# Summing attention and graph-convolution blocks of edges with one scan each instead of one vector operation per edge

## What is computed

```
L0: segment_sum(exp(-w)[:, None] * x[dst], src)
L1: MLP over segment_sum, max and mean of edge_attr_32 by src
L2: twice   h = x @ W
            out = segment_sum(h[src] * norm[:, None], dst) + b
L3: attention, 4 heads of 16:
    attn = leaky_relu(a_src[src] + a_dst[dst] + edge_attr @ W_edge)
    attn = exp(attn - max over dst);  attn /= sum over dst
    out  = segment_sum(h[src] * attn, dst)
```

## Time and profile before

| | |
|---|---|
| median of 3 timed runs | 10099.72 us |
| span of the profiled execution | 11181.7 us |
| busy in it: POOL, DVE, PE, ACT | 7106.9, 4736.9, 1801.6, 1142.1 us |
| ranking pass, first to last scatter issue | 511.8 to 2881.5 us |
| c1, first to last gather issue | 3850.1 to 6017.3 us |
| c2, first to last gather issue | 6222.7 to 8389.4 us |
| attention, first to last gather issue | 8707.2 to 10966.1 us |

### The profile page before, as it was taken

One profiled execution on the slowest core, in us unless ns is written; L12 is line 12 of the kernel. 1 busy time (PEld: TensorE's weight loads), 2 busy tenths in 40 slices (PEclk: granted clock), 3 DMA queues, 4 the chain that ended last, 5 costly groups with the idle time before them and its releaser, 6 DMA issues.

```text
span 11181.7 us, 57120 instructions
## 1 busy us (share of the span) xinstructions
PE 1801.6 (16%) x9285; PEld 1516.5 (14%) x9285; DVE 4736.9 (42%) x20005; ACT 1142.1 (10%) x2728; POOL 7106.9 (64%) x6884
## 2 busy tenths in 40 slices
PE   8744444444000400000000000000001000000000
PEld 7633333333000300000000000000000000000000
DVE  8855555555797422222221222222224344444446
ACT  0143434343000100000000000000000000000000
POOL 0566666666201377777776677777777776666766
PEclk7755555555555555555555555555555555555555
DMA  5144444444575111111111111111111222222221
GB/s 224 57 129 122 129 124 126 124 127 122 204 273 203 32 50 46 48 46 48 46 48 37 50 46 48 46 48 46 48 46 30 54 53 58 53 58 55 56 55 44
DMA packets 570444, 911.29 MB, mean 81 GB/s; under 512 B 333435, under 2 KB 348228, under 8 KB 544824
## 3 DMA queue, kind: packets, MB, share of 16 engines
q1 hardware_dynamic: 350264, 652.74, 17.3%
q0 software_dynamic: 219904, 255.88, 10.8%
HBM read 494.12 MB, written 414.02 MB: 81 GB/s over the span
## 4 chain that ended last, share of the span: by engine, by line
DVE 34%; issue 28%; another core or an unknown queue 17%; POOL 16%; PE 3%; DMA 1%; ACT 1%; DVEq 0%; SPq 0%; POOLq 0%; ACTq 0%
DVE arena_a L1495 16%; POOL arena_a L641 15%; DVE arena_b L1112 4%; DVE arena_a L1110 3%; DVE arena_b L1125 3%; DVE arena_a L1425 3%; POOL arena_a L610 2%; PE bank L811 2%; DVE arena_b L1056 1%; DVE arena_b L1093 1%; PE bank L916 1%; DVE arena_a L1625 0%; PE bank L890 0%; DMA arena_a<-in_a 0%
## 5 line engine op out<-in xcount | busy, mean ns | idle before, releaser
L641 POOL DMA_INDIRECT arena_a<-table_c,decay x3136 | 3284.6, 1047 | 1257.6 <-issue 1051.2
L1495 DVE SCALAR_TENSOR_TENSOR arena_a<-arena_a,same_dst 128x64 f32<-128x64 f32 x3134 | 891.5, 284 | 3449.5 <-DVE arena_a L1495 2713.2
L591 POOL DMA_INDIRECT by_src<-arena_b,idx_blk x1568 | 1570.8, 1002 | 885.8 <-issue 449.4
L641 POOL DMA_INDIRECT arena_a<-table_at,decay x1568 | 1556.8, 993 | 703.8 <-issue 468.4
L1110 DVE SCALAR_TENSOR_TENSOR arena_a<-arena_a,same_dst 128x64 f32<-128x64 f32 x1567 | 441.9, 282 | 711.1 <-remote 547.7
L864 PE MATMUL bank<-ident,chunk_end 128*64 128x128 f32 (+2 forms) x8 | 2.7, 442 | 4416.0 <-DVEq L973 4416.0
L864 PEld LDWEIGHTS bank<-ident,chunk_end 128*64 128x64 f32 (+2 forms) x8 | 1.4, 240 | 4416.6 <-DVEq L973 4416.6
L1112 DVE SCALAR_TENSOR_TENSOR arena_b<-arena_a,src_f,before 128x128 bf16<-128x128 f32 x1568 | 543.7, 347 | 37.4 <-issue 37.4
L850 PE MATMUL bank<-hrows 98*128 98x128 f32 x1568 | 404.0, 440 | 659.5 <-DVE arena_b L1125 331.9
L850 PE MATMUL bank<-hrows,arena_a 98*128 98x128 f32 x1568 | 403.3, 438 | 658.0 <-DVE arena_b L1125 347.4
L753 ACT ACTIVATE arena_b<-arena_a,decay 128x64 f32<-128x64 f32 x1568 | 394.2, 334 | 972.5 <-remote 610.2
(11 more groups left out here) (279 smaller groups left out, 4845.9 us busy)
## 6 DMA issues: line engine op xcount, KB each, us to landing
arena_a<-ids_rows SPq DMA_DIRECT2D x98, 1024.0 KB
states_src<-arena_a SPq DMA_DIRECT2D x98, 1024.0 KB
states_c<-arena_a SPq DMA_DIRECT2D x196, 512.0 KB
hrows<-by_src SPq DMA_DIRECT2D x98, 776.0 KB, 6.1
states_at<-arena_a SPq DMA_DIRECT2D x98, 576.0 KB
x_at_start<-arena_a SPq DMA_DIRECT2D x7, 7168.0 KB, 49.0
arena_a<-x_at_start SPq DMA_DIRECT2D x98, 512.0 KB
arena_a<-table_c,decay POOLq DMA_INDIRECT x3136
```

Source lines behind the costliest of these rows:

```text
L591: pool.indirect_dma_start(out=by_src, out_offset=AT(ap=idx_blk[r][:, k:k + 1], axis=0), in_=rows[r][:, k, :], in_offset=None)\
L641: pool.indirect_dma_start(out=gb[r][:, k * w:(k + 1) * w], out_offset=None, in_=table[g], in_offset=AT(ap=src_i[:, n * J + k:n * J + k + 1 ...
L1495: ins = v.scalar_tensor_tensor(out=st[h][:, k * D:(k + 1) * D], in0=old, scalar=same_dst[:, e:e + 1], in1=gb[r][:, k * D:(k + 1) * D], op0 ...
```

## The change

Every block of the three passes is now laid out feature by feature: 64 (c1, c2) or 68 (attention) rows of J + 1 = 17 slots. Slot 0 holds what is carried from the block before, slots 1 to 16 the edges; a mask of the same layout holds same_dst in slots 1 to 16 and 0 in slot 0, so that one TENSOR_TENSOR_SCAN over all 64 * 17 = 1088 or 68 * 17 = 1156 columns starts again at each feature. The buffers `in0`, `in1`, `mask0`, `mask1` lie at the end of arena_b, `sums0`, `sums1` in arena_a.

In c1 and c2, ACT spreads the mask (`mask_spread`, 1024 columns), turns the gathered block from edge-major to feature-major (1024 columns) and, after the scan, turns the sums back into `st` (`rows_back`, 1024 columns). DVE does one scan and one copy of 64 columns that carries the last slot over. POOL waits for `row_turned` of ACT instead of `state`. In attention the weighing writes the feature-major order itself, the exponentials of ACT go straight to it, POOL waits for `weighed`, the scan takes the place of the 33 operations, and steps 0 to 2 of the next block's scores (step 2 waits for the next block's gathers) are issued before it, steps 3 to 6 behind it. The products `run` are gone.

```diff
-        run = {2 ** level: digits[o, w][:, :].bitcast(f32)[:, 0:NBLK * J // 2]...
+        by_feature = carve(arena_b[:, KN * W01 - 4 * W3 * (J + 1):],
+                           [(f"{name}{h}", W3 * (J + 1)) for name in ("mask", "in") for h in range(2)])
...
+        def features(name, w):
+            return by_feature[name][:, 0:w * (J + 1)].rearrange("p (f j) -> p f j", j=J + 1)
...
-                    if n >= R:
-                        pool.wait_ge(s("state"), upto(g, "state") + n - R + 1)
+                    if n >= R and g == "at":
+                        pool.wait_ge(s("weighed"), n - R + 1)
+                    elif n >= R:
+                        pool.wait_ge(s("row_turned"), upto(g, "row_turned") + n - R + 1)
...
+        def mask_spread(act, g, n):
+            w = W3 if g == "at" else D
+            if n >= 2:
+                act.wait_ge(s("summed"), upto(g, "summed") + n - 1)
+            act.activation(features(f"mask{n % 2}", w)[:, :, 1:J + 1], bf(same_dst[:, n * J:(n + 1) * J], w), ACT.Copy)\
+               .then_inc(s("mask_spread"), 1)
+
+        def rows_back(act, g, n):
+            w, row = (W3, W3S) if g == "at" else (D, D)
+            act.wait_ge(s("summed"), upto(g, "summed") + n + 1)
+            if n >= 2:
+                act.wait_ge(s(f"stored{n % 2}"), upto(g, f"stored{n % 2}") + 16 * (n // 2))
+            act.activation(st[n % 2][:, 0:J * row].rearrange("p (j f) -> p j f", f=row)[:, :, 0:w],
+                           features(f"sums{n % 2}", w)[:, :, 1:J + 1].rearrange("p f j -> p j f"), ACT.Copy)\
+               .then_inc(s("state"), 1)
+
+        def conv_act(act, g):
+            act.wait_ge(s("masks_zeroed"), 1)
+            for n in range(NBLK):
+                r = n % R
+                mask_spread(act, g, n)
+                act.wait_ge(s(f"gathered{r}"), upto(g, f"gathered{r}") + (n // R + 1) * (16 * J))
+                act.activation(features(f"in{n % 2}", D)[:, :, 1:J + 1],
+                               gb[r][:, 0:J * D].rearrange("p (j f) -> p f j", f=D), ACT.Copy)\
+                   .then_inc(s("row_turned"), 1)
+                if n:
+                    rows_back(act, g, n - 1)
+            rows_back(act, g, NBLK - 1)
...
-                    for k in range(J):
...
-                        ins = v.scalar_tensor_tensor(out=st[h][:, k * D:(k + 1) * D], in0=old,
...
+                    v.wait_ge(s("mask_spread"), upto(g, "mask_spread") + n + 1)
+                    v.wait_ge(s("row_turned"), upto(g, "row_turned") + n + 1)
+                    flat = slice(0, D * (J + 1))
+                    v.tensor_tensor_scan(by_feature[f"sums{h}"][:, flat], by_feature[f"mask{h}"][:, flat],
+                                         by_feature[f"in{h}"][:, flat], 0.0, ALU.mult, ALU.add).then_inc(s("summed"), 1)
+                    if n + 1 < NBLK:
+                        v.wait_ge(s("summed"), upto(g, "summed") + n + 1)
+                        v.tensor_copy(features(f"in{1 - h}", D)[:, :, 0], features(f"sums{h}", D)[:, :, J])\
+                            .then_inc(s("row_carried"), 1)
...
-                hview = by_head(g3)[:, :, :, 0:HD]
-                v.tensor_tensor(hview, hview, ex_e.rearrange("p j (c o) -> p j c o", o=1)
+                v.tensor_tensor(weighed(n)[:, :, 0:HD, 1:J + 1].rearrange("p c d j -> p j c d"),
+                                by_head(g3)[:, :, :, 0:HD], ex_e.rearrange("p j (c o) -> p j c o", o=1)
                                 .to_broadcast([P, J, HEADS, HD]), ALU.mult).then_inc(s("weighed"), 1)
                 if ahead:
-                    score_step(n + 1, 0)
+                    for step in range(3):
+                        score_step(n + 1, step)
                 v.wait_ge(s("weighed"), n + 1)
-                sums_of(n, g3, late["tmp"], s3[:, :, 0:W3], n + 1 if ahead else None)
+                if n >= 2:
+                    v.wait_ge(s("state"), upto("at", "state") + n - 1)
+                v.tensor_tensor_scan(by_feature[f"sums{h}"], by_feature[f"mask{h}"], by_feature[f"in{h}"], 0.0,
+                                     ALU.mult, ALU.add).then_inc(s("summed"), 1)
+                if ahead:
+                    for step in range(3, 7):
+                        score_step(n + 1, step)
```

More of the change, by code:

```diff
@@ L59 @@
 ORDER = dict.fromkeys(ADDED, PASSES)
-ORDER.update(dict.fromkeys((*(f"gathered{r}" for r in range(R)), "table", "table_out", "chain"),
-                           CONVS))
+ORDER.update(dict.fromkeys((*(f"gathered{r}" for r in range(R)), "table", "table_out", "row_turned", "row_carried",
+                            "mask_spread", "summed"), CONVS))
 ORDER.update(dict.fromkeys(("onehots", "onehots_used"), ("dst", "src")))
@@ L1416, in _ @@
             tell("table")
[L1418 to L1440, removed]
-                    for k in ks:
-                        if k // span % 2:
-                            last = join(k, made[:, k // span * span - 1, :],
-                                        run[span][:, n, k // (2 * span) * span + k % span:][:, 0:1], k % span == 0)
-                    return last
-                def score(step):
-                    if scored:
-                        score_step(scored, step)
-                first, second = range(half), range(half, J)
-                joined("first", join(0, carried, same_dst[:, e:e + 1], True))
-                joined("second", pairs(range(half + 1, J, 2)))
-                pairs(range(3, half, 2))
-                score(1)
-                after_half("first")
-                joined("first", join(1, made[:, 0, :], same_dst[:, e + 1:e + 2], True))
-                after_half("second")
-                joined("second", level(2, second))
-                score(2)
-                after_half("first")
-                joined("first", level(2, first))
-                after_half("second")
-                joined("second", level(4, second))
-                score(3)
-                after_half("first")
-                joined("first", level(4, first))
-                score(4)
-                after_half("second")
-                after_half("first")
-                level(half, range(half, half + 4))
-                score(5)
-                level(half, range(half + 4, J)).then_inc(s("state"), 1)
-                score(6)
@@ L1521, in conv_nodes @@
                 link(v.tensor_tensor(rows3, rows3, per_node(dinv, p, D), ALU.mult))
-            for span, product in run.items():
-                uppers = same_dst[:, :].rearrange("p (m two k) -> p m two k", two=2, k=span)[:, :, 1, :]
-                to = product.rearrange("p n (m k) -> p (n m) k", k=span)
-                link(v.tensor_copy(to, uppers))
-                for k in range(1, span):
-                    link(v.tensor_tensor(to[:, :, k], to[:, :, k], to[:, :, k - 1], ALU.mult))
+            for h in range(2):
+                link(v.memset(by_feature[f"mask{h}"], 0.0))
+            tell("masks_zeroed")
             conv("c1")
@@ L1565, in _ @@
             link(v.memset(late["mx"], 0.0))
-            for h in range(2):
-                link(v.memset(msk[h], 0.0))
             tell("at_begun")
```

71 lines of the change are left out of this document (26 added, 45 removed).

## The result

| | before | after |
|---|---|---|
| median of 4 timed runs | 10099.69 us | 10624.1 us |
| lowest to highest | 10092.31 to 10106.65 | 10619.74 to 10627.47 |

The changed kernel is slower: ratio 1.052, 95% interval 1.0505 to 1.0535, or 524 us. The profiled execution of after took 10624.95 us and its span is 10622.7 us. The profile of before had a span of 11181.7 us. Profiled again in experiment 1, the same kernel has a span of 10104.8 us, and experiments 9 to 11 meet a chip on which it takes 11112.54 us; most likely the profile of before comes from such a chip, though its chip isn't on record.

The account below looks back on a forecast made before the run. The prediction took POOL's issuing of indirect transfers to bound all three passes. Its terms, 382 + 143 - 3 = +522 us on 10099.7, gave 10620 us (5.2% slower), with a range of 10400 to 10800.

Parts of the forecast that it names:

- the pace of 1.40 us: In the profile of before, a dependent DVE step every 1.40 us instead of 0.32; claimed absent from timed runs.
- Term 1: c1 and c2: removing DVE's chain of 16 steps, 5.1 us a block, is worth nothing; likewise attention's 33 operations.
- Term 2: ACT in c1 and c2: three operations of 1.13 us, 3.4 us of a 20 us block, covered even at 7 us.
- the prediction's own sign: Check on ACT's work: its estimate is wrong if an ACT operation takes over 2 us.
- Term 3, c1 and c2: The long scan holds a POOL gather issued under it: 1.95 us a block in 196 blocks, +382 us.
- Term 3, attention: The scan holds a gather for 1.7 us, short operations give back 0.24: 1.46 in 98 blocks, +143 us.
- Term 4: Moved waits of POOL and the carry copy after the scan: 0, at most 0.15 us a block, 44 us in all.
- Term 5: Ends of passes: nothing in c1 and c2, -3 us in attention.
- The profiled execution: The profiled span should fall by about 140 us, to 11040, while timed runs get slower.
- Rival A: DVE's slow pace is real in timed runs and the change frees it: 9960 us, or 9770 at lower losses; 10%.
- Rival B: The lock between DVE and POOL costs nothing here, only the ends of passes count: 10097 us; 5%.
- C: ACT becomes the bound, three turned operations above 20 us a block; at 24 us a block, 10880 us; 2%.

Follow-up runs that it names:

- experiment 1: The kernel before, unchanged, profiled once more: profiled execution 10106.58 us, span 10104.8 us, beside a timed median of 10099.15 us.
- experiments 9 to 11: Before with weighing in 8 pieces; that plus ranking one-hots in 4 each; after with all these and its scans cut: 11192.75, 11276.76, 11192.71 us.
- experiment 2: After, with a second scan of 1088 columns on constants behind the first in each c1 and c2 block: 10828.97 us, ratio 1.0723 to before.
- experiment 4: After, with the scan of c1 and c2 cut into 8 pieces of 136 columns: 10319.06 us, ratio 1.0215 to before.
- experiment 6: After, with an ACT operation on 840 constant columns ahead of each turning in c1 and c2, delaying the scan: 10524.2 us, ratio 1.0428 to before.
- experiment 3: After, with two one-input TENSOR_REDUCE of 1216 columns added in each c1 and c2 block: 10623.58 us, ratio 1.052 to before.
- experiment 11: After, with both scans and the weighing cut, and the ranking pass's one-hots in 4 pieces each: 11192.71 us, ratio 1.0081 to before.
- experiment 8: After, with the c1 and c2 scan in 8 pieces, attention's scan in 17 and the weighing in 8: 10062.19 us, ratio 0.9971 to before.
- experiment 5: After, with an ACT operation on 400 constant columns ahead of each turning in c1 and c2: 10603.74 us, ratio 1.0509 to before.

## Why the prediction was right, step by step

*What bounds the kernel.* Right for the timed runs: POOL issues without a pause at 20.03 us a block in c1 and c2, 20.8 in attention (said: 20.0 and 20.7). The way to it was not sound. I took the pace of 1.40 us for the work of recording one execution, because the profiled span was 1082 us above the median. Most likely the two did not come from like chips: on the chip of experiments 9 to 11 all executions take 11104 to 11296 us, profiled or not, and on the others profile and time agree at about 10100 for before. The count of where the 1082 us lie was of use even so, since it said how the kernel runs without the pace: said were 207, 207, 223 and up to 332 us for c1, c2, attention and the ranking pass, and experiment 1 has them 205, 205, 220 and 310 us shorter than the earlier trace rows. The rule of the Trainium skill ("NOTIFIC — the notification-queue block", 7.1) that I put beside it is neither borne out nor refuted: profiled executions of experiment 1 and of after are as fast as the timed ones, and what makes the pace on the other chip no run here shows.

*Term 1*, DVE's chain is worth nothing: right, DVE waits 15 us a block for data in experiment 1.

*Term 2*, ACT: too low. By the prediction's own sign, an operation of over 2 us, it is wrong. Turning takes 1.94 us, not 1.13; `rows_back` 2.0 (2037 ns in the group's mean); only spreading the mask, which turns nothing, takes 1.05. I had said that even twice as much, 7 us, is covered, and it is: 5 us of 21.7. But it moved the phase.

*Term 3, c1 and c2*: the mechanism is right (experiments 2, 4 and 6, and the rows beside experiment 3), the size was 382 us and is 331. The scan is as long as said (2.43 against 2.48 us). The step that was off is where it starts: "some 3.7 us after that issue, and POOL issues at 3.75". With a turning of 1.94 it misses that issue and starts 0.5 us ahead of the one behind it, so 1.74 us are lost and not 2.0. The error in term 2 gave 50 us back.

*Term 3, attention*: 143 us said, 187 measured; per block 1.46 us, and 2.74 less the 0.84 that before has in experiment 1, so 1.90. The scan costs 1.35 us a block, less than the 1.7 I took. What was missing is the weighing: I had it at 1.22 us and 0.45 lost (0.38 in experiment 1), unchanged, but with its strided output it takes 1.94 us and 1.27 are lost. It is named in the change (the weighing writes the new order), and I costed only where it writes, not how.

*Term 4*, waits moved: right at 0. POOL's idle time is the same as before, and no wait for a buffer shows in it.

*Term 5*, ends: right. From the last gather of attention to the end of the span, after takes 3.9 us less than experiment 1 (said: 3), and all that isn't in the gathers comes to under 1 us.

*The sum*: +522 said, +524 measured. Two errors of some 50 us each, of opposite sign, make that closeness luck; the mechanism and its bounds are what held.

*The profiled execution*: I had its span fall to 11040. It was taken on a chip without the pace, so its span of 10622.7 us neither confirms nor refutes it.

*Rival A* has changed its meaning. The pace is real in timed runs, on one chip of the four. The changed kernel itself never ran there. Its premise, that DVE's steps set 22.1, falls with experiment 11, where they are gone and the pass takes as long. *Rival B* falls with 1.74 us lost a block and with experiment 4; *C* with ACT idle for 16.7 us of a block.

## What to carry to other kernels

Where GpSimd's issuing of indirect transfers is the bound, the length of each single VectorE instruction with two SBUF inputs is a cost of its own: a short chain with gaps beats one long instruction, even when VectorE's total goes down. Cutting the long ones into pieces of 0.3 to 0.4 us took back all of it in sum (experiment 8). Price a stride by its own row, since it made a copy and a product of 1024 columns 1.6 to 1.9 times as long (1.94 or 2.0 against 1.05 us, 1.94 against 1.22). And where a profile's span and the timed median differ by more than a few us, suspect that they come from different chips, and compare the same kernel's profile and time on one.

## What was not expected of the hardware

- One chip of the four ran the kernel before in 11112.5 us, the others in 10085 to 10100. There, 16 gathers take 22.1 us, not 20.0, whether VectorE makes 16 dependent steps or a scan in 8 pieces.
- A held gather loses what is left of the operation less 0.19 us under a scan, less 0.12 under the weighing of before and 0.24 under that of after: 1.91 left and 1.73 lost in after, 1.55 and 1.36 in experiment 6, 1.27 and 1.07 in experiment 2, 2.35 and 2.15 in experiment 5.
- A gather running when a scan starts doesn't lengthen the scan, and isn't lengthened by it (2.42 us and 0.94 us in after and in experiment 6).
- Some 0.01 us of phase can decide 1.1 us: delaying the scan by 0.42 us split the blocks into two kinds, by a start before or after 4.945 us from the block's last issue, in place of making all of them dearer. Which kind a block is doesn't follow that of the block before it.
